# A state-space mixer's prologue rewritten: x projected once and convolved by channel, tables from powers

## The reference

```
xz = hidden @ W_in.T ; x, z = split            # 256 channels each
x  = silu(conv1d(x, conv_w, 4 taps, causal) + conv_b)
dtA = exp(log_dt) * (-exp(log_A_real) + 1j*A_imag)         # 256 x 8 states
Ct = (C_re + 1j*C_im) * (exp(dtA) - 1) / A
k[h, l] = 2 * Re(sum_n Ct[h, n] * exp(dtA[h, n] * l))      # 512 long
y  = causal convolution of x with k, + D * x
y  = y * silu(z) ; mixer = y @ W_out
x  = layernorm(hidden + mixer)
e  = argmax of 8 gate logits ; x = layernorm(x + expert_e(x))   # 128-512-128, relu
```

## Time and profile before

| | us |
|---|---|
| median of 3 runs | 266.92 |
| lowest, highest | 265.96, 268.56 |
| span of the profiled execution, first to last instruction | 263.8 |
| TensorE, VectorE, ScalarE, GpSimd busy in it | 239.2, 177.0, 187.1, 139.8 |

### The profile page before, as it was taken

The page is one execution under the profiler, slowest core; times in us unless marked ns, Lnnn a source line. Parts: engine busy times, 40 slices in busy tenths (PEclk is TensorE's granted clock), DMA queues, the critical chain, the costliest instruction groups (busy, mean ns, idle before and its releaser), DMA issues.

```text
span 263.8 us, 8892 instructions
## 1 busy us (share of the span) xinstructions
PE 239.2 (91%) x2763; PEld 215.1 (82%) x2764; DVE 177.0 (67%) x552; ACT 187.1 (71%) x528; POOL 139.8 (53%) x208
## 2 busy tenths in 40 slices
PE   8999979999999899999979999359989999999970
PEld 4888768888887678888869999349979999899960
DVE  1889995997218657777724878842877676566672
ACT  2999999856998778888655665207667777667740
POOL 6000000400009989999624687878746656657545
PEclk9999999999999999999999999759999999999995
DMA  7697884600399999999293221647865676677600
GB/s 232 180 313 288 346 334 150 244 0 0 105 310 332 310 279 296 308 320 302 66 361 120 93 93 41 212 92 191 220 179 172 200 210 164 203 195 208 189 34 6
DMA packets 54267, 52.06 MB, mean 197 GB/s; under 512 B 4415, under 2 KB 42817, under 8 KB 54114
## 3 DMA queue, kind: packets, MB, share of 16 engines
q1 hardware_dynamic: 51506, 46.65, 59.2%
q0 software_dynamic: 2304, 4.34, 4.6%
q10 hardware_dynamic: 432, 0.79, 0.8%
HBM read 38.14 MB, written 14.07 MB: 198 GB/s over the span
## 4 chain that ended last, share of the span: by engine, by line
PE 59%; DVE 10%; ACT 10%; POOL 9%; issue 6%; DMA 5%; SPq 1%; DVEq 0%; ACTq 0%; POOLq 0%
PE banks L1292 13%; PE banks L1477 9%; PE banks L1487 8%; PE banks L1370 7%; POOL dispatched_rows L568 5%; ACT BR L672 5%; PE banks L1380 5%; PE banks L1384 4%; PE banks L1275 3%; PE banks L1357 3%; PE banks L1435 2%; DMA X<-dispatched_rows 2%; POOL RE L558 1%; DMA out<-X 1%; POOL out L576 1%
## 5 line engine op out<-in xcount | busy, mean ns | idle before, releaser
L515 POOL TENSOR_TENSOR Wx<-BR,RE 128x384 f32 (+1 forms) x32 | 47.9, 1548 | 27.9 <-PE banks L1292 26.6
L1292 PE MATMUL banks<-Wx,XT 128*128 128x256 f32 x256 | 59.9, 380 | 1.7 <-ACT Z L643 1.7
L809 ACT ACTIVATE Z<-banks,BR 128x128 f32<-128x128 f32 x156 | 44.6, 368 | 18.4 <-PE banks L1477 18.3
L1292 PEld LDWEIGHTS banks<-Wx,XT 128*128 128x128 f32 x256 | 48.4, 190 | 9.0 <-issue 2.2
L576 POOL DMA_INDIRECT out<-X x39 | 38.4, 986 | 27.8 <-DVE X L1233 15.3
L1477 PE MATMUL banks<-Z 128*128 128x128 f32 x312 | 42.7, 281 | 0.4 <-ACT Z L798 0.2
L1487 PE MATMUL banks<-BR,Z 128*128 x312 | 41.1, 276 | 1.2 <-DVE X L1216 1.2
L1477 PEld LDWEIGHTS banks<-Z 128*128 128x128 f32 x312 | 39.0, 196 | 1.0 <-issue 0.5
L1487 PEld LDWEIGHTS banks<-BR,Z 128*128 128x128 f32 x312 | 37.8, 192 | 1.5 <-issue 1.5
L568 POOL DMA_INDIRECT dispatched_rows<-TR,CR x32 | 31.0, 970 | 9.3 <-POOL RE L558 9.3
L1057 DVE TENSOR_TENSOR X<-banks,Z 128x256 f32 (+1 forms) x32 | 20.4, 636 | 9.1 <-PE banks L1384 9.1
(11 more groups left out here) (220 smaller groups left out, 469.6 us busy)
## 6 DMA issues: line engine op xcount, KB each, us to landing
TR<-kernel_rows SPq DMA_DIRECT2D x32, 512.0 KB, 6.5
Z<-w SPq DMA_DIRECT2D x39, 256.0 KB, 3.1
dispatched_rows<-TR SPq DMA_DIRECT2D x3, 2310.0 KB, 8.8
X<-dispatched_rows SPq DMA_DIRECT2D x39, 66.0 KB, 2.1
XT<-hidden_t SPq DMA_DIRECT2D x10, 256.0 KB, 3.1
RE<-decay_and_turns SPq DMA_DIRECT2D x2, 1024.0 KB, 7.4
BR<-w SPq DMA_DIRECT2D x1, 2048.0 KB, 8.2
dispatched_rows<-TR SPq DMA_DIRECT2D x1, 1848.0 KB, 7.8
```

The lines of the kernel that those rows point to most:

```text
L515: nc.gpsimd.tensor_tensor(BC[:, k, 0:LAGS, :].rearrange("p m (s r n) -> p (m s) r n", s=STRIPS, r=2), Btab[:, :, :, :, :, one].rearrange(" ...
L809: last = nc.scalar.activation(HT[:, j, c * P:c * P + P], bank[UP_BANKS[j]][:, c * P:c * P + P], ACT.Relu, bias=B1[:, bass.ds(experts[j] * ...
L1292: last = mm(bank[X_BANKS[k]][:, j * CHAN:(j + 1) * CHAN], XT[:, slot, at:at + CHUNK], Wx[:, tap, :], start=(tap == 0), stop=(tap == TAPS - 1))
```

## The change

x is projected once, channels on the partitions: two batches of 128 channels at a time, two products of 512 columns (`project_x`, eight times). ScalarE makes the last tap and the bias on the way out of PSUM (`last_tap`), VectorE adds the other three taps from PSUM with three shifted passes (`add_taps`), TensorE turns the result (`turn_x`, eight transposes), ScalarE stores it (`keep_x`). The gates go through banks 6 and 7 a batch at a time, and Silu is applied when they are copied (`keep_z`); `gate_silu` is gone.

For the tables 28 angles a state are taken (16 fine steps, 8 coarse ones, 3 lags, a half step), one Exp and two Sin over all of them. Etab is the product of coarse and fine powers on VectorE (`expand`). The state weight and the lags go into a small turning matrix made on POOL (Rot), and TensorE multiplies: Btab = Etab times Rot, 14 half rounds of ten products (the last two of four), each of 32 rows by 128 weight columns by 96 columns, into banks 6 and 7 (`state_tables`), copied by ScalarE (`keep_states`). POOL's product in the groups becomes a copy. The DRAM round trip of decays and turns goes; the fills of the dispatch rows are issued ahead of the batch loads.

```diff
+            def project_x(i):
+                j = i % 2
+                wait_past(pe, s_xk, (i - 1) * LAGS)
+                for k in range(2):
+                    b = i // 2 * 2 + k
+                    pe.wait_ge(s_xt[b % A_BATCH], (b // A_BATCH + 1) * 16)
+                    last = mm(bank[i % 2 * 2 + k][:, :], Win[:, j * P:(j + 1) * P], XT[:, b % A_BATCH, :], start=True, stop=True)
+                last.then_inc(s_x, 1)
+
+            def project_gates(b):
+                pe.wait_ge(s_xt[b % A_BATCH], (b // A_BATCH + 1) * 16)
+                wait_past(pe, s_z, b)
+                for k in range(CHUNKS):
+                    last = mm(bank[6 + k // 2][:, k % 2 * CHAN:(k % 2 + 1) * CHAN], XT[:, b % A_BATCH, k * P:(k + 1) * P],
+                              Win[:, CHAN:], start=True, stop=True)
+                last.then_inc(s_zp, 1)
+
+            def turn_x(i):
+                pe.wait_ge(s_xk, (i + 1) * LAGS)
+                wait_past(pe, s_xe, i)
+                for k in range(2):
+                    for chunk in range(CHUNKS):
+                        at = slice(chunk * P, (chunk + 1) * P)
+                        last = nc.tensor.transpose(bank[4 + k][:, at], xc[:, i % 2, k, at], ident[:, :])
+                last.then_inc(s_xtr, 1)
+
+            def state_tables(h):
+                at, half = h // 2 * ROUND, h % 2
+                count = min(ROUND, GROUPS - at)
+                if h == 0:
+                    pe.wait_ge(s_kx, 1)
+                wait_past(pe, s_bt, h)
+                pe.wait_ge(s_rot, 1 if at + count <= GROUPS // 2 else 2)
+                for g in range(count):
+                    for k in range(2):
+                        rows = slice((half * 2 + k) * STRIP, (half * 2 + k + 1) * STRIP)
+                        last = mm(bank[6 + k][:, g * LAGS * STRIP:(g + 1) * LAGS * STRIP], Etab[rows, at + g, :], Rot[rows, at + g, :],
+                                  start=True, stop=True)
+                last.then_inc(s_b, 1)
...
+            project_x(0)
+            project_x(1)
+            project_gates(0)
+            project_gates(1)
+            pe.wait_ge(s_const, 2)
+            turn_x(0)
+            project_x(2)
+            project_gates(2)
+            turn_x(1)
+            project_x(3)
+            for b in range(3, BATCH):
+                project_gates(b)
+
+            pe.wait_ge(s_z, BATCH)
+            pe.wait_ge(s_sel, 1)
+            pe.wait_ge(s_c, 2)
...
             last.then_inc(s_kp, 1)
...
+            turn_x(2)
+            project_x(4)
+            for h in range(0, 3):
+                state_tables(h)
+            turn_x(3)
+            project_x(5)
+            for h in range(3, 6):
+                state_tables(h)
...
```

ScalarE and VectorE:

```diff
+            def last_tap(i):
+                j = i % 2
+                act.wait_ge(s_x, i + 1)
+                wait_past(act, s_xtr, i - 1)
+                nc.scalar.activation(xc[:, i % 2, :, :], pair_banks(i % 2 * 2), ACT.Identity,
+                                     scale=channel[:, j, TAPS - 1:TAPS], bias=channel[:, j, TAPS:TAPS + 1]).then_inc(s_x3, 1)
+
+            def keep_x(i):
+                j, b = i % 2, i // 2 * 2
+                act.wait_ge(s_xtr, i + 1)
+                for k in range(2):
+                    last = nc.scalar.activation(x_tiles[:, b + k, :, j * P:(j + 1) * P],
+                                                bank[4 + k][:, :].rearrange("p (k c) -> p k c", k=CHUNKS), ACT.Copy)
+                last.then_inc(s_xe, 1)
+
+            def keep_z(b):
+                act.wait_ge(s_zp, b + 1)
+                nc.scalar.activation(z_tiles[:, b, :, :],
+                                     banks[:, 6 * 512:8 * 512].rearrange("p (k c) -> p k c", k=CHUNKS), ACT.Silu).then_inc(s_z, 1)
+
+            def keep_states(h):
+                at, half = h // 2 * ROUND, h % 2
+                count = min(ROUND, GROUPS - at)
+                act.wait_ge(s_b, h + 1)
+                nc.scalar.activation(Btab[:, at:at + count, half * 2:half * 2 + 2, :].rearrange("p g s c -> p s g c"),
+                                     pair_banks(6)[:, :, 0:count * LAGS * STRIP].rearrange("p s (g c) -> p s g c", g=count),
+                                     ACT.Copy).then_inc(s_bt, 1)
...
+            last_tap(0)
+            last_tap(1)
+            keep_z(0)
+            keep_z(1)
+            keep_x(0)
+            last_tap(2)
+            keep_z(2)
+            keep_x(1)
+            last_tap(3)
+            for b in range(3, BATCH):
+                keep_z(b)
+            keep_x(2)
+            last_tap(4)
+            for h in range(0, 3):
+                keep_states(h)
+            keep_x(3)
+            last_tap(5)
...
+            def add_taps(i):
+                j, slot = i % 2, i % 2
+                dve.wait_ge(s_x3, i + 1)
+                for back in range(1, TAPS):
+                    if back > 1:
+                        dve.wait_ge(s_xk, i * LAGS + back - 1)
+                    stt(xc[:, slot, :, back:], pair_banks(i)[:, :, 0:SEQ - back], channel[:, j, TAPS - 1 - back:TAPS - back],
+                        xc[:, slot, :, back:], ALU.mult, ALU.add).then_inc(s_xk, 1)
...
+            def group_tables(r, k):
...
-                nc.gpsimd.tensor_tensor(
...
+                nc.gpsimd.tensor_copy(BC[:, k, 0:LAGS * P],
+                                      Btab[:, bass.ds(g, 1), :, :].rearrange("p g s c -> p (g s c)")).then_inc(s_bc, 1)
```

More of the change, by code:

```diff
@@ L22 @@
 TILES = TOKENS // P
-PAIRS = TILES // 2
 GH = 8
@@ new lines, in build, with angles @@
+        second = BR[:, 0:4096]
+        angle_home = BR[:, 8192:]
+        def angles(at):
+            return angle_home[:, at * GROUPS * ANGLES:(at + 1) * GROUPS * ANGLES].rearrange("p (g a) -> p g a", g=GROUPS)
+        fall, sine, cosine = angles(0), angles(1), angles(2)
+        coarse_home = angle_home[:, 3 * GROUPS * ANGLES:]
+        coarse_part, first_coarse, second_coarse = [
+            coarse_home[:, at * GROUPS * COARSE:(at + 1) * GROUPS * COARSE].rearrange("p (g b) -> p g b", g=GROUPS)
+            for at in range(3)]
@@ L710, in group_input @@
+            keep_x(4)
+            last_tap(6)
+            for h in range(6, 8):
+                keep_states(h)
+            keep_x(5)
+            last_tap(7)
+            for h in range(8, 10):
+                keep_states(h)
+            keep_x(6)
+            for h in range(10, 12):
+                keep_states(h)
+            keep_x(7)
+            for h in range(12, HALF_ROUNDS):
+                keep_states(h)
             def group_input(r, k):
@@ new lines, in _ @@
+            dve.wait_ge(s_ch, 16)
+            add_taps(0)
+            add_taps(1)
+            products = second.rearrange("p (g i) -> p g i", g=GROUPS)
+            halves = (slice(0, GROUPS // 2), slice(GROUPS // 2, GROUPS))
+            for part in halves:
+                expand(Etab[:, part, :], part, first_coarse, cosine)
+                done(expand(products[:, part, :], part, second_coarse, sine))
+                tt(Etab[:, part, :], Etab[:, part, :], products[:, part, :], ALU.add).then_inc(s_c, 1)
@@ L1336, in _ @@
                         g = half * 16 + strip * 4 + q
[L1337 removed]
+                        last = mm(bank[6][strip * 32:strip * 32 + 32, half * CHUNK:(half + 1) * CHUNK], Sel[:, g, :], Etab[:, g, :],
                                   start=(q == 0), stop=(q == 3))
             last.then_inc(s_kp, 1)
[L1340 to L1341 removed]
+            turn_x(2)
@@ L1345, in sum_states @@
+            turn_x(7)
+            for h in range(12, HALF_ROUNDS):
+                state_tables(h)
             def sum_states(r, k):
```

692 lines of the change are left out of this document (255 added, 437 removed).

## The result

The changed kernel took 285.04 us (median of 5 runs, 283.42 to 290.7) beside 266.96 for the kernel before (5 runs, 265.96 to 268.57). The ratio is 1.064, 95% interval 1.058 to 1.070: slower by 6.4%, about 17 us. The forecast was 269.3 with a range to 283; the time lies above both.

The account below looks back on a forecast made before the run. TensorE, full until the first group at 80.04 us, was taken as the bound. Start 16.6, gates to 42.5, state tables to 82.6: +2.6, less 0.2 for POOL's copy, gave 266.2 span, 269.3 us; range 261 to 283.

Parts of the forecast that it names:

- rival (c): TensorE from 42 us on: clock stays down in short bursts with 1.3 us gaps, some 19 us more, 288; chance 0.10.
- one fall of the clock: TensorE after idling before 16.6 us: first product at half speed, 1.8 us extra, granted clock full afterwards.
- the row of 136 to 138: Trace window before the change: TensorE busy 1.16 of 2 us, clock 1.00, cited against the clock staying down.
- the ring: State tables: TensorE's half rounds wait for ScalarE's copies; seven bare waits of 0.27, 0.94 and 0.08, 9.0 us.
- The half round: State tables: ten products, twenty passes, two weight loads at once, 1.07 us; twelve such and two of 0.43, 13.7 us.
- Rival (b): Half rounds: weight loads go one by one, 2.13 us each, first group at 95.9, time 282.5; chance 0.20.
- rival (a): Half rounds at the state sums' pitch, 0.26 us, and no clock fall at 16.6: 261.2 us; chance 0.25.
- The kernel rows: 64 small products behind the gates, ahead of the state tables: forecast to start at 42.5 us, taking 1.96.
- the ladder: Gates of the last four batches, one at a time through banks 6 and 7: 3.08 us each, 12.3 to 42.5.
- The start: Parameters, tables, first projections, last taps and keep_z(0), ending at 16.6 us, when gates(1) can go.
- The groups: 32 groups at a pitch of 1.47 us, TensorE's work unchanged, other engines' changes hidden: costed at nothing.
- the 6 us of cover: VectorE beside the gates: six Etab passes of 2.3 us to 36.1, add_taps(2) to 39.8, off the path.

Follow-up runs that it names:

- e2: Changed kernel with ten more unread 32-row products in each of eight waits for a copied half round: 279.62 us, executions too far apart for a ratio.
- e3: Changed kernel with each half round as five products over all 128 rows instead of ten over 32, tables wrong, waits left empty: 275.29 us, ratio 1.023.
- e4: Changed kernel with some half rounds put into banks 4 and 5 instead of 6 and 7, so two run back to back: 269.74 us, ratio 0.998.
- e1: Changed kernel with two unread 256-column products over the whole array in each of eight waits for a copied half round: 272.66 us, ratio 1.012.
- e5: Changed kernel with twelve unread 256-column products in TensorE's idle time before gates(1): 283.14 us, ratio 1.053.
- e11: e9 with the banks of a block's two half rounds exchanged, one half round before turn_x(7) and five behind it: 263.8 us, ratio 0.985.
- e9: e8 with half rounds spread two to a block, the last four behind turn_x(7), and three unread products at the end: 274.53 us, ratio 1.017.
- e12: e11 without any unread filler product: 264.55 us, ratio 0.986.
- e6: e4 with gates(4) and gates(6) in banks 4 and 5 instead of 6 and 7: 271.09 us, ratio 1.014.
- e8: e6 with the filler of e5 and four more unread products, one before the 13th half round and three behind the last: 267.57 us, ratio 0.998.

## Why the prediction was wrong

**The failed step** is rival (c) and the 0.10 it was given: "TensorE's clock falls and stays down while it works in short bursts with gaps of 1.3 us". Its price was some 19 us more, 288 us in all; the runs took 283.4 to 290.7. The forecast assumed one fall of the clock, and the profile has it at 0.64 on average from 48 to 100, worth 14.0 us there. That (c)'s first group (82.6 and 19, 101.6) is so near the 100.41 measured is in part luck: 3.8 of the 17.8 us between are a path that is longer at full clock too, and behind the first group came 4.5 us that no rival had. I had set the row of 136 to 138 against it, busy 1.16 of 2 us at a clock of 1.00, as if the busy time told the level. The windows of e2 and e3 show that it doesn't. The products at 136 were not looked at: they are the transposes L1418, over all rows, with 0.84 us of idle time, where the row of 168 has 2.70 before it and the ring was to have 1.3. A half round, on 32 of 128 rows, had no row of its like in the kernel before. With that admitted, (c) should have had a third of the chance or more, and the range should have reached 290.

The Trainium skill (TensorE: Matmul & The Clock Gate, A second HAM failure mode) was the rule that I weighed and set aside; it gave the right result. The trace agrees with it in outline, with waits of 1.07 us for banks and a clock that swings. Waits of 1.21 us between the gates (28 to 44 us) left the clock at 1.00, though.

**The half round was right.** The forecast's 1.07 us to the last product, and 0.27 more until the reader starts, are 1.34 against 1.36; two in a row take 2.12 (e4). That is 0.053 us a pass; e3's ten passes over all rows, with the same 96 columns, take 1.25 to 1.35 us, twice as much a pass. Rival (b), one load after another, would be 2.13 a half round and falls. The Trainium skill (same page, Packing small matmuls) has a weight load overlap with products in flight only where these are on another strip of rows, and the trace agrees. The idle time was 1.07 and not 1.29, since the 1.36 holds the 0.27. The sums' pitch of rival (a) was not reached either.

**The rest of the forecast, at full clock,** can be read from e1: first group at 86.43 where the forecast had 82.6. The kernel rows were 0.8 to 1.2 us late (43.34, in e1 43.68, forecast 42.5): four batches of the ladder took 3.17 and not 3.08 each, and most of turn_x(0) was at half clock as well, 1.48 us to the next start where I had 0.88. From the first half round to the first group e1 took 38.1 us, the forecast 35.5: a pitch of 2.43 and not 2.36, 1.81 from start to start for x(i) and 1.20 for its last tap where I had 1.73 and 1.08, and the ends of the ring. So at full clock the forecast was 3.8 us short, and the state tables' clock added 12 to 14.

**The start was nearly right**: gates(1) at half clock (3.75 us where e5 has 1.89, forecast 1.8 us extra) and at 16.58 (forecast 16.6), with turn_x(0) as the part left out. In e5's trace 1.9 us of it reach the kernel rows; that they reach the end the runs do not show.

**The groups** were costed at nothing, and took 4.5 us more. ScalarE's L753 went from 0.42 to 0.66 us and hid, as was said. But each profile has one or two stalls of TensorE on its own instructions among the first groups: 0.26 and 0.95 us before, 0.24 and 1.94 after, 1.71 and 0.84 in e4, and 0.35 alone in e11. In the changed kernel the long one was followed by a group at half clock, which took 2.6 us. From the first Toeplitz product to that of the last group it is 52.5 us against 48.0; at 31 times 1.47 both would be 45.6. Of the 6.9 us over it, 2.8 are the state stage's clock carried over (three groups at 2.62, 2.62 and 1.95), and 3.7 are the stall of 1.94 and what is at half clock behind it. The kernel before has 2.4 over it. Why the stall is longer in some programs stays open: no experiment moved it by itself.

**Also open** is what decides when the clock falls. In e9 the same wait was passed three times and the clock fell in the fourth, and the executions of e2 lie 8 us apart. Full-array products in the waits (e1) and fewer or shorter waits (e4, e11, e12) kept it up, but in e6, whose waits there are e4's, it fell at 63, and in e11 at 74, behind 4.39 us of 32-row products and a wait of 0.46. How much the rows count is not shown.

## What to carry to other kernels

TensorE's granted clock belongs in the forecast of every change that takes TensorE from full to waiting: for the stretch that is to wait, work out the time at both levels, and take the lower one as a likely case if the products and waits to come have no row of their like in the trace. Before a busy share is read as harmless, look at which products it is of and how long they waited. Before an engine's work is cut, look at what its waits will be bound to. Here 41 us of products went, and what was left was a ring of single-buffered banks; two bank pairs took the ratio to the kernel before from 1.064 to 0.998, and the order in which the copies free them, with what e6 to e8 added, on to 0.985. A free wait can hold a full-array product with no reader, which in e1 cost nothing and kept the clock.

## What was not expected of the hardware

- TensorE's busy share and its clock went apart in both directions. From 76 to 80 us of e9 it was busy 4.00 of 4 us at 0.50, more than half of it with 32-row products; from 48 to 52 of e3 it was busy 1.87 of 4 at 1.00.
- VectorE's products of 2048 elements out of two tensors took 3.84 and 4.88 us beside POOL's L559 (which ended at 28.98), and the next two, with POOL idle, 2.28 each:

```profile
21.37 7.61 POOL L559 TENSOR_TENSOR RE<-RE,same_state 128x1536 f32<-128x1536 f32 x2
...
22.48 3.84 DVE L937 TENSOR_TENSOR CR<-BR 128x2048 f32<-128x2048 f32 x1
...
33.38 2.28 DVE L937 TENSOR_TENSOR CR<-BR 128x2048 f32<-128x2048 f32 x1
```

  The forecast had 2.3 for each of the six passes; the exponential table was done at 40.1 and not at 36.1, which took 4 of the 6 us of cover. It didn't reach the path in the changed kernel, but with the quicker ladder of e6 the kernel rows waited for that table.
- ScalarE's 256 elements with other strides (L753, read and written) took 0.66 us and not 0.42. VectorE's gate product, with other strides too, went the other way: 0.425 us (L975) where L1057 took 0.638.
